# Other instruction orders at the start and at both borders of attention, norms in parts and on GpSimd, and operands at multiples of 128 bytes, in a macaron block on one core

## What is computed

```python
def _anemll_linear(x, w, su, sv):
    return jnp.einsum('bsh,oh->bso', x, w * (su @ sv))
def _L0_ffn_ref(x, ...):                      # 1792 inner channels
    a = _anemll_linear(x, gate_w, gate_su, gate_sv)
    b = _anemll_linear(x, up_w, up_su, up_sv)
    return _anemll_linear(jax.nn.silu(a) * b, down_w, down_su, down_sv)
def _L0_attn_ref(x, Wq, Wk, Wv, Wo, q_norm_w, k_norm_w):   # 32 heads of 128, 8 key/value heads
    q, k = _rmsnorm(q, q_norm_w), _rmsnorm(k, k_norm_w)
    scores = jnp.einsum('bkgqd,bksd->bkgqs', qg, k) / math.sqrt(HD)
    bias = jnp.where(rel > 0, NEG_INF, slopes[:, :, None, None] * rel)
    attn = jax.nn.softmax(scores + bias[None], axis=-1)
    return jnp.einsum('bkgqs,bksd->bkgqd', attn, v)... @ Wo.T
x = x + 0.5 * _L0_ffn_ref(_layernorm(x), ...)
x = x + _L0_attn_ref(_layernorm(x), ...)
x = x + 0.5 * _L0_ffn_ref(_layernorm(x), ...)
```

## Time and profile before

| what | value |
|---|---|
| median of 3 runs | 1319.01 us (1317.69 to 1319.38) |
| the profiled execution | 1320.19 us, its span 1318.9 us, mean granted TensorE clock 0.993 |
| PE busy | 1280.4 us, 97% of the span, 6694 instructions |
| PEld | 1090.8 us, 83% |
| DVE | 723.9 us, 55% |
| ACT | 668.3 us, 51% |
| POOL | 395.4 us, 30% |
| chain that ended last | PE 94%, DVE 3%, ACT 1%, issue 1% |

### The profile page before, as it was taken

One profiled execution on the slowest core, in us unless ns is written; L12 is line 12 of the kernel. 1 busy time (PEld: TensorE's weight loads), 2 busy tenths in 40 slices (PEclk: granted clock), 3 DMA queues, 4 the chain that ended last, 5 costly groups with the idle time before them and its releaser, 6 DMA issues.

```text
span 1318.9 us, 18154 instructions
## 1 busy us (share of the span) xinstructions
PE 1280.4 (97%) x6694; PEld 1090.8 (83%) x6694; DVE 723.9 (55%) x1911; ACT 668.3 (51%) x1623; POOL 395.4 (30%) x326
## 2 busy tenths in 40 slices
PE   5999999999999999999999999999999779999999
PEld 4888888788888888888888888888888667888887
DVE  7444444676666665665665665665666754333333
ACT  4222222348657657657657657657656642222221
POOL 4222222634224224224224224224223201222220
PEclk9999999999999999999999999999999989999999
DMA  7022222101101001001001101001001010111111
GB/s 265 33 99 99 99 99 99 48 1 49 33 1 49 33 1 49 33 1 49 33 1 48 33 1 49 33 1 49 33 1 49 0 48 1 48 48 49 48 48 64
DMA packets 15015, 60.18 MB, mean 46 GB/s; under 512 B 2064, under 2 KB 2736, under 8 KB 12880
## 3 DMA queue, kind: packets, MB, share of 16 engines
q1 hardware_dynamic: 14928, 59.02, 12.3%
HBM read 45.91 MB, written 13.11 MB: 45 GB/s over the span
## 4 chain that ended last, share of the span: by engine, by line
PE 94%; DVE 3%; ACT 1%; issue 1%; SPq 0%; DMA 0%; DVEq 0%
PE bank L179 29%; PE bank L181 28%; PE bank L180 28%; PE bank L302 5%; PE bank L281 2%; PE bank L203 1%; ACT prob L480 1%; DVE stats L588 1%; PE bank L284 0%; DMA fac_raw_down<-ffn_fac 0%; PE bank L194 0%; DVE probT_l L719 0%; DVE xnT_lo L624 0%; DVE x_rows L641 0%; PE bank L189 0%
## 5 line engine op out<-in xcount | busy, mean ns | idle before, releaser
L480 ACT ACTIVATE prob<-prob,neg_top 128x128 f32<-128x128 f32 (+3 forms) x256 | 140.9, 552 | 78.7 <-DVE neg_top L708 78.1
L847 POOL TENSOR_TENSOR rows<-rows,row_root_y 128x640 f32<-128x640 f32 x64 | 80.5, 1258 | 272.9 <-DVE row_root_y L584 272.9
L494 ACT CAST probT_h<-bank 128x512 fp32r<-128x512 f32 x160 | 84.5, 596 | 152.3 <-PE bank L302 152.3
L812 POOL TENSOR_TENSOR w_l_late<-raw_late,w_h_late 128x512 fp32r<-128x512 f32 (+1 forms) x64 | 93.7, 1485 | 205.8 <-ACT w_h_late L396 205.8
L632 DVE TENSOR_TENSOR d<-bank,silu 128x512 f32<-128x512 f32 x56 | 38.7, 691 | 208.0 <-PE bank L181 203.9
L841 POOL TENSOR_TENSOR square<-rows 128x640 f32<-128x640 f32 x64 | 80.3, 1255 | 209.0 <-ACT rows L459 208.9
L488 ACT ACTIVATE prob<-prob,inverse 128x128 f32<-128x128 f32 (+3 forms) x256 | 123.0, 554 | 0.2 <-DVE inverse L713 0.2
L179 PE MATMUL bank<-w_h_late,xnT_hi 128*128 128x512 f32 (+1 forms) x352 | 121.6, 346 | 0.0
L181 PE MATMUL bank<-w_h_late,xnT_lo 128*128 128x512 f32 (+1 forms) x352 | 118.9, 338 | 0.0
L180 PE MATMUL bank<-w_l_late,xnT_hi 128*128 128x512 f32 (+1 forms) x352 | 118.5, 337 | 0.0
L719 DVE TENSOR_TENSOR probT_l<-bank,probT_h 128x512 fp32r<-128x512 f32 x160 | 101.5, 685 | 26.4 <-ACT probT_h L494 26.4
(11 more groups left out here) (120 smaller groups left out, 3398.8 us busy)
## 6 DMA issues: line engine op xcount, KB each, us to landing
raw_late<-w_qkv SPq DMA_DIRECT2D x8, 1536.0 KB, 6.4
raw_early<-ffn_w SPq DMA_DIRECT2D x21, 512.0 KB, 5.0
scaled<-raw_early SPq DMA_DIRECT2D x21, 512.0 KB, 2.6
raw_late<-scaled SPq DMA_DIRECT2D x21, 512.0 KB, 4.6
raw_late<-w_o SPq DMA_DIRECT2D x8, 1024.0 KB, 4.7
x_rows<-x SPq DMA_DIRECT2D x8, 256.0 KB, 5.1
y<-x_rows SPq DMA_DIRECT2D x8, 256.0 KB, 2.0
fac_raw_gu<-ffn_fac SPq DMA_DIRECT2D x14, 32.0 KB, 3.4
```

What stands on the lines that cost most here:

```text
L480: last = act.activation(p, p, ACT.Exp, bias=neg_top[:, h:h + 1], scale=-1.0, accum_out=total[:, h:h + 1])
L494: act.copy(probT_h[:, j, :, :], banks[r.bank][:, :].rearrange("p (h q) -> p h q", h=G)).then_inc(probT_hi_done, 1)
L812: return pool.tensor_tensor(lo, raw, hi.bitcast(F32), ALU.subtract)
L847: pool.tensor_tensor(row, row, by, ALU.mult).then_inc(rows_normed, 1)
```

## The change

Five things are changed.

1. **Start.** ScalarE's queue, not SyncE's, issues the loads of `lo_rows`, of the first factors and of x blocks 2 and 3. The parts of `fix` are made in two halves with semaphores of their own, the first half ahead of the first factors. Of the four norms of b=0, VectorE does blocks 0 and 1 and GpSimd blocks 2 and 3. ScalarE copies the first transposed block between the two halves of the first weights. A new function `ffn_first` orders the first step of both passes: gate c=0 b=0, gate c=1 b=0, the transposes of b=1, down b=0, gate c=0 b=1.
2. **Entry to attention.** In the last step of the first pass gate c=1 b=1 stands ahead of down b=0. `from_ffn_to_attention` then interleaves down b=1, the norms and transposes of b=0 in two halves, the projections of units 0 to 3, and puts all transposes of b=1 behind `turn_rows(0)`.
3. **Slots.** The statistics of the output rows are taken out of `project_out` and stand a slot later (`output_statistics`). Where t = 1, ScalarE takes the exponentials of two heads, evacuates the values of the unit before, and takes the other two.
4. **Exit.** `normal_roots` of b=0 moves from slot 61 to slot 62, its norms go to GpSimd behind the last slot, and slot 63 holds neither transposes of x nor the half gate group. Behind it stand the values of unit 63, the transposes of b=0, the output projection of 63 and `ffn_first(1)`.
5. **Layout.** `sums` moves behind `oT_l`, so that `v_h` to `oT_l` lie 64 bytes lower, at multiples of 128.

The diff, cut to its core:

```diff
@@ tiles
         o_h, o_l = sb("o_h", [G, DM], F32R), sb("o_l", [G, DM], F32R)
-        sums = sb("sums", [2, G + 1])
         v_h, v_l = sb("v_h", [B, TB, HD], F32R), sb("v_l", [B, TB, HD], F32R)
...
         oT_h, oT_l = sb("oT_h", [G, P], F32R), sb("oT_l", [G, P], F32R)
+        sums = sb("sums", [2, G + 1])
@@ TensorE
+            def ffn_first(p):
+                gate_up(p, 0, 0, 0)
+                gate_up(p, 0, 1, 0)
+                turn_normed(2 * p, 1)
+                down(p, 0, 0)
+                gate_up(p, 0, 0, 1)
+                if p == 0:
+                    scale_weights(1, "gu0")
...
+            def from_ffn_to_attention():
+                down(0, STEPS - 1, 1, (0, 1))
+                turn_normed(1, 0, (0, 1))
+                down(0, STEPS - 1, 1, (2, 3))
+                for n in range(LEAD):
+                    project(n, "q")
+                    project(n, "kv")
+                    if n == 0:
+                        turn_normed(1, 0, (2, 3))
+                turn_rows(0)
+                turn_normed(1, 1)
...
                 if n:
                     project_out(n - 1)
-                if n == UNITS - 1:
-                    turn_normed(2, 0)
-                    gate_up(1, 0, 0, 0, (0,))
                 turn_probabilities(n)
...
             for n in range(UNITS):
                 slot(n)
-            gate_up(1, 0, 0, 0, (1,))
             weigh_values(UNITS - 1)
-            gate_up(1, 0, 1, 0)
+            turn_normed(2, 0)
             project_out(UNITS - 1)
-            down(1, 0, 0)
-            turn_normed(2, 1)
-            gate_up(1, 0, 0, 1)
+            ffn_first(1)
@@ ScalarE
+            def load_first():
+                act.dma_start(lo_rows, factor_lo).then_inc(fix_in, 16)
+                act.dma_start(fac_raw["gu0"], ffn_fac[0, 0]).then_inc(fac_in["gu0"], 16)
+                for t in range(2, TB):
+                    act.dma_start(xr[:, t, :], x_rows[t]).then_inc(x_in[t], 16)
...
+                soon = G // 2 if unit(n)[2] == 1 else G
+                exponentials(n, range(soon))
                 if n:
                     weigh_values(n - 1)
+                exponentials(n, range(soon, G))
...
+            scale_weights(0, 0, "gu0", (0,))
+            turn_normed(0, 0, (0,))
+            scale_weights(0, 0, "gu0", (1,))
+            turn_normed(0, 0, (1, 2, 3))
@@ VectorE
+            def ffn_first(p):
+                if p == 0:
+                    normalize(0, 1)
+                gate_up(p, 0, 0, 0)
+                if p == 1:
+                    normalize(2, 1)
+                gate_up(p, 0, 1, 0)
+                turn_normed(2 * p, 1)
+                down(p, 0, 0)
+                gate_up(p, 0, 0, 1)
...
+            def from_ffn_to_attention():
+                last = STEPS - 1
+                down(0, last, 0, (0, 1))
+                normal_roots(1, 0, (0, 1))
+                normalize(1, 0, (0, 1))
+                down(0, last, 0, (2, 3))
+                turn_normed(1, 0, (0, 1))
+                normal_roots(1, 0, (2, 3))
+                normalize(1, 0, (2, 3))
+                down(0, last, 1, (0, 1))
+                values_lo(0)
+                turn_normed(1, 0, (2, 3))
+                down(0, last, 1, (2, 3))
+                values_lo(1)
+                sum_squares(0)
+                sum_squares(1)
+                pair_roots(0)
+                normal_roots(1, 1)
+                normalize(1, 1)
...
+                turn_rows(0)
+                turn_normed(1, 1)
...
                 if n == UNITS - 2:
-                    normalize(2, 0)
+                    normal_roots(2, 0)
                 if n + 1 < UNITS:
                     turn_rows(n + 1)
-                if n == UNITS - 3:
-                    normal_roots(0)
+                if unit(n - 2)[0] == HKV - 1:
+                    output_statistics(n - 2)
...
-                if n == UNITS - 1:
-                    normal_roots(1, range(TB - 1))
-                    turn_normed(2, 0)
                 turn_probabilities(n)
...
-            normalize(0, 0)
+            normalize(0, 0, (0, 1))
...
+            turn_normed(2, 0)
             project_out(UNITS - 1)
+            output_statistics(UNITS - 2)
+            output_statistics(UNITS - 1)
+            normal_roots(2, 1)
+            ffn_first(1)
@@ GpSimd
+            def normalize(L, b, blocks=range(TB)):
+                pool.wait_ge(ln_root_done, LN_ORDER.index((L, b, 0)) + 1)
+                for t in blocks:
...
+                    pool.tensor_scalar(xn[:, t, :], xr[:, b * TB + t, :], mv[:, b * TB + t, 0:1], ln_root[:, t:t + 1],
+                                       ALU.subtract, ALU.mult).then_inc(xn_pool_done, 1)
...
+            normalize(0, 0, (2, 3))
             for kind in KINDS:
                 scale_weights(0, 0, kind)
...
+            normalize(2, 0)
             ffn(1)
@@ SyncE
-            for t in range(TB):
+            for t in range(2):
                 sp.dma_start(xr[:, t, :], x_rows[t]).then_inc(x_in[t], 16)
```

236 lines of the change are left out of this document (116 added, 120 removed).

## The result

The changed kernel takes 1310.53 us (median of 4 runs, 1310.03 to 1312.67) against 1318.74 us for the kernel before, measured with it: a ratio of 0.9942, 95% interval 0.9924 to 0.9959. The forecast was 1302.8 us with a range of 1296.0 to 1310.5. The direction was right; the gain was 8.2 us where 16.2 were forecast, and the time lies just outside the range.

A forecast was written before the change was run, and what follows sets the result against it. Bound by PE's idle stretches at start, entry and exit of attention, and its matmul pace in the middle. 1320.2-2.7 (start)+2.5 (entry)-4.5 (middle)-11.5 (exit) = 1304.0, median 1.2 lower: 1302.8 us, range 1296 to 1310.5.

The forecast's parts named there:

- the gate at 18.4: Start: first gate matmul 7.3 us after the roots, with x 0.2 us earlier, against 18.75 before.
- the new wait for the factors: Start: second scaling waits 1.05 us for factors queued on GpSimd behind two low parts.
- the wait in front of down: Start: down needs both gated products, which VectorE finishes late; TensorE waits 1.7 us.
- the argument from the row at 272.96: Start: VectorE's op started 0.04 us before GpSimd's yet waited, so norms are not halved; gate 7.3 us after roots, not 7.0.
- Rival 2: Entry: GpSimd does not hold the root steps; 3.6 us less, 1299.2 us; chance 0.10.
- The fall of the clock: Entry: PE idle some 3 us, clock may halve, mostly hidden by the wait behind; loss 2.3, with the clock 2.5 us.
- rival 1: Middle: project_out's slow pace has another cause than the offset; 4.5 us more, 1307.3 us; chance 0.20.
- the changes between kinds of pairs: Middle: switching between aligned and offset operand pairs costs a few slow steps, some 13 ns a unit, 0.8 us.
- 0, bounds 0.5 either way: Middle: split exponentials where t=1 only change when ScalarE copies oT_h, so nothing moves; 0 us.
- The count of work from the output projection of unit 62 on: Exit: from its end to the end of b=1's first gate group 33.55 us instead of 43.1, 9.55 gained.
- Rival 4: Start and exit: GpSimd norms cost much more than its other ops; slower than before from 5.75 us a norm; chance 0.04.
- Rival 3: Exit: a wait stays, for instance values for probT_l, with a fall of the clock; 1306 to 1308 us; chance 0.12.

The follow-up runs named there:

- e3_norms_on_vector: Changed kernel with all four norms of b=0 at the start on VectorE instead of two on GpSimd; median 1311.09 us (1307.38 to 1315.45).
- run 427: Not a follow-up run: the words say that matmuls of 512 columns at the start are spaced 427 ns apart.
- e11_exit_norms_vector: Changed kernel with the four norms of b=0 at the exit on VectorE behind slot 63 instead of on GpSimd; median 1310.37 us (1309.04 to 1310.92).

## Why the prediction was wrong in size

The stages miss their forecasts by 4.2, 0.7 and 3.6 us for the worse and 1.7 for the better, 6.8 together; the step from trace to median adds the last 1.0.

**The start (4.2 us off): the step that failed is the gate at 18.4.** Three of its parts were wrong. The loads: x was taken to land 0.2 us earlier, and the last block landed late, so that the roots ended at 12.20 instead of 11.10. VectorE's statistics of that block begin at 7.28 to 7.47 in the four traces with the old loads and at 7.82 to 9.44 in the twelve with the new ones. The queue: the norms were counted from the end of the roots, though the order rows printed in the part on the change show three factor instructions ahead of them on GpSimd, and the trace of before shows GpSimd at those factors only at 13.20 and 14.70. The sum has no term for when GpSimd would come to the norms. The price: 1.4 us for a norm from rows of 1.25 and 1.49, where it takes 2.06. The rows of before:

```profile
13.20 0.72 POOL L812 TENSOR_TENSOR fac_gu<-fac_raw_gu,fac_gu 32x256 fp32r<-32x256 f32 x1 [3.54 <-ACT fac_gu L381]
...
14.70 0.72 POOL L812 TENSOR_TENSOR fac_down<-fac_raw_down,fac_down 32x256 fp32r<-32x256 f32 x1 [0.78 <-ACT fac_down L381]
```

Behind the gate 32.7 us passed to the second scaling against 32.25 by the sum, but that is luck: the new wait for the factors was 0.84 us (1.05 forecast) and the wait in front of down 0.53 us and not 1.7, and what these two saved went to the gate's first matmuls at 427 ns, some 1.4 us in 48 matmuls (12.31 for 10.9) that the sum does not have.

On how the two engines share, the argument from the row at 272.96 was too pessimistic for the first norm: TensorE's transposes began at 12.89, 0.69 us after it started, against 0.60 before. That norm took 0.55 us, and GpSimd's instruction, which started 0.16 us behind it, 0.96 where the same took 0.72 in the kernel before. The rule of the Trainium skill (SBUF — State Buffer, Who interferes with whom) that the first to issue has the ports agrees with these rows. It does not fit the row of before, where VectorE's first norm started 0.04 us ahead and took 1.57 us of the 2.94; with starts so close the case is open.

**The entry (0.7 us off): right by its own steps.** The four slow root steps came at 1.04, 1.18, 1.17 and 1.25 us, the roots ended 39.5 us after the stage's start for 39.05 forecast, the first scores at 43.6 for 43.0. Rival 2, the steps not held, is out. The fall of the clock was hidden, as forecast.

**The middle (3.6 us off).** The mechanism of the layout was right, and rival 1 is out; its term, 4.5 us, measured 3.3. Of this the changes between kinds of pairs are as forecast (0.9 us in the projections for 0.8), and project_out is the part that was mis-sized: 3.7 us forecast for the 64 units, 2.5 measured in 58 of them, since the first five of a group's eleven steps (228 to 236 ns) are no faster than before, which leaves about half of the 5.0, not 3.7. The larger part of the miss is the exponentials, **the second step that failed:** "0, bounds 0.5 either way" was -2.4 us. The step looked at who takes oT_h and not at what covered the reciprocal: before, in slot 9, ScalarE copied oT_h at 397.55, VectorE's reciprocal ran at 397.68 under it, and the probabilities followed at 398.01 without a wait:

```profile
397.55 0.57 ACT L499 CAST oT_h<-bank 128x512 fp32r<-128x512 f32 x1
397.68 0.18 DVE L713 RECIPROCAL inverse<-total 128x4 f32<-128x4 f32 x1 [0.38 <-ACT prob L480]
398.01 1.71 ACT L488 ACTIVATE prob<-prob,inverse 128x256 f32<-128x256 f32 x4
```

Put ahead of the last two exponentials, the copy covers nothing. 0.36 us in 7 slots is 2.5 us, because in these slots the low parts of o are waited for; in the slots with t=1 of b=1, with the same split, nothing moved.

**The exit (1.7 us better).** The count of work from the output projection of unit 62 on gave 33.55 and it took 33.7. What was left out is that the output projection itself took 4.45 us at the half clock before and takes 2.87 now. Rival 4 had the right sign on GpSimd's price but not its size: 2.06 us against the 5.75 where it would have decided. Rival 3, a wait that stays with a fall of the clock, is there in part: the wait for probT_l is 0.18 us, those for oT_l stay at 1.75 to 2.15, and a half-clock stretch of 3.4 us behind one of them stays, worth 1.5 us by the table.

The range was too narrow: the bounds of the start were on the price of a norm and on the loads, none on when a queue would reach it, and those of the exponentials, 0.5 us either way, were on a term that was put at nothing.

Three small sums of the prediction are off and decide nothing: 10.4 and two products of 2.05 are 14.5, not 14.35; 6.92 less 5.92 is 1.00, not 1.05; and rival 4 at a norm of 7 us comes to 1326.5, not 1326.8.

## What to carry to other kernels

Work that moves to another engine starts when that engine's queue comes to it, not when its input is ready: read what stands ahead in the order and when its loads land, then count. An evacuation that looks misplaced may be what covers another engine's short answer. And try the parts of a change apart: here two of five cost 5.5 us of what the others gained, and without these and with the old loads and norms the gain is 15.9 us instead of 8.2.

## What the runs showed of the hardware

- A GpSimd tensor_scalar with two operations of 128x512 fp32 takes 2.06 us, VectorE's 0.48 (1.92 for four).
- Two fp32r operands of a matmul of which one lies at a multiple of 128 bytes and the other 64 past one cost 3 to 4 ns in each of project_out's matmuls of 512 columns (229.8 against 233.7 and 233.8 ns). Other distances were not tried. The Trainium skill (TensorE: Matmul & The Clock Gate, Back-to-back issue gap) has no term for an address; the runs with one operand off disagree with it by this much.
- TensorE's clock falls to its half level (1.2 of 2.4 GHz) behind waits, for 3.4, 6.8 or 10.2 us in these traces, and whether it does differs between executions of one kernel: the four runs of e3_norms_on_vector took 1307.4, 1307.6, 1314.6 and 1315.5 us, the first two at a mean clock of 0.997 and the others at 0.991. At the exit 3.4 us of it cost 1.5 us (278.3 against 279.8), at the entry nothing (244.90 against 244.91), where TensorE waits 2.92 us at that place. A change that is worth less than this shows in the lengths of stages, not in the total of a few runs.
- At the start matmuls of 512 columns run 427 ns apart, the pace of the half level, until some point that moves from trace to trace (25.1 us in the changed kernel, 22.2 in e11_exit_norms_vector), while the granted clock of the windows reads 1.00: there the spacing has to be read, not the clock.
